# Preparing the quantised weight with fp32 matmuls on TensorE in place of GpSimd and VectorE arithmetic, in a one-core attention and feed-forward kernel

## The reference, cut to what matters

```
x = x + causal_attention(q = LN(x), k = ctx, v = ctx)          # 16 heads of 64
mask   = sigmoid(mask_weight)                                  # [4]
soft   = sigmoid(pweight) - sigmoid(nweight)                   # [1024 out, 1024 in, 4]
weight = einsum('oin,n->oi', soft, exps * mask) * scale[0]
bias   = quantise(einsum('on,n->o', pbias - nbias, bexps)) * biasscale[0]
x = x + LN(x) @ weight.T + bias
```

## Time and profile before

| what | value |
|---|---|
| median of 3 runs (lowest to highest) | 1310.44 us (1309.8 to 1312.69) |
| profiled execution, its own time | 1313.67 us |
| its span in the trace | 1310.7 us |
| mean granted TensorE clock, share of full speed | 0.944 |
| TensorE matmul busy (share of the span) | 1144.8 us (87%) |
| VectorE busy | 1072.6 us (82%) |
| ScalarE busy | 926.6 us (71%) |
| GpSimd busy | 599.9 us (46%) |
| read from memory, written to it | 67.15 MB, 16.78 MB |

### The profile page before, as it was taken

How to read it: one execution, slowest core, us unless ns; L and a number is a source line. 1 busy time by engine, 2 the same in 40 slices (tenths; PEclk the granted TensorE clock), 3 DMA queues, 4 the chain that set the end, 5 groups by cost and what they waited for, 6 DMA issues and landing times.

```text
span 1310.7 us, 28652 instructions
## 1 busy us (share of the span) xinstructions
PE 1144.8 (87%) x11088; PEld 848.5 (65%) x11088; DVE 1072.6 (82%) x1613; ACT 926.6 (71%) x2011; POOL 599.9 (46%) x717
## 2 busy tenths in 40 slices
PE   1555665589998999999999999999999999999998
PEld 1433444466766677777777677787776677777753
DVE  3588998878897688888898898888988888888861
ACT  1677787567776577777777777777787777777740
POOL 2378666533324574433324954433237744332241
PEclk9867767689999999999999999999999999999999
DMA  6899899243333675433324856434226854320113
GB/s 187 224 223 255 225 267 240 66 106 89 66 81 69 158 168 123 114 81 93 72 82 82 201 121 130 97 82 94 70 64 147 178 116 111 81 66 2 33 41 89
DMA packets 245622, 157.08 MB, mean 120 GB/s; under 512 B 220912, under 2 KB 220912, under 8 KB 245488
## 3 DMA queue, kind: packets, MB, share of 16 engines
q1 hardware_dynamic: 245488, 155.26, 49.5%
HBM read 67.15 MB, written 16.78 MB: 64 GB/s over the span
## 4 chain that ended last, share of the span: by engine, by line
PE 62%; DVE 19%; issue 6%; ACT 5%; POOL 3%; DMA 3%; SPq 1%; ACTq 0%; DVEq 0%; POOLq 0%
PE ffnb L433 20%; PE ptb L401 14%; PE oacc L415 7%; PE slot L388 7%; PE slot L389 7%; DVE pt_lo L570 5%; PE oacc L417 4%; DVE stats L584 3%; DVE mx L563 3%; ACT pt_hi L476 2%; PE slot L433 2%; PE slot L392 2%; DMA qt<-q 1%; DVE y L610 1%; DVE ring L619 1%
## 5 line engine op out<-in xcount | busy, mean ns | idle before, releaser
L570 DVE SCALAR_TENSOR_TENSOR pt_lo<-ptb,pt_hi 128x384 f16<-128x384 f32 (+2 forms) x688 | 382.9, 597 | 117.6 <-ACT pt_hi L476 115.4
L466 ACT ACTIVATE p<-slot,mx 128x512 f32<-128x512 f32 (+7 forms) x512 | 378.0, 747 | 96.1 <-DVE mx L563 94.1
L476 ACT ACTIVATE pt_hi<-ptb 128x384 f16<-128x384 f32 (+2 forms) x688 | 326.4, 527 | 150.2 <-PE ptb L401 149.4
L401 PE MATMUL ptb<-id,p 128*128 128x128 f32 x2304 | 340.8, 289 | 75.9 <-DVE pt_lo L570 75.0
L563 DVE TENSOR_REDUCE mx<-slot 128x1 f32<-128x640 f32 (+7 forms) x352 | 359.5, 1021 | 32.8 <-PE slot L392 30.2
L433 PE MATMUL ffnb<-wt,yt 128*128 128x512 f16 x1440 | 365.3, 381 | 18.6 <-DVE ring L619 15.6
L401 PEld LDWEIGHTS ptb<-id,p 128*128 128x128 f32 x2304 | 259.5, 146 | 87.6 <-issue 84.4
L388 PE MATMUL slot<-kt,qt 128*128 128x128 f16 (+3 forms) x1056 | 278.5, 293 | 38.8 <-DMA qs<-qt 26.5
L753 POOL TENSOR_TENSOR att<-osb 128x256 f32<-128x256 f32 x128 | 98.8, 772 | 398.9 <-ACT osb L483 375.8
L389 PE MATMUL slot<-kt,qs 128*128 128x128 f16 (+3 forms) x1056 | 278.4, 293 | 0.0
L415 PE MATMUL oacc<-v,pt_hi 128*128 128x128 f16 x2304 | 252.3, 224 | 15.3 <-ACT osb L483 13.4
(11 more groups left out here) (64 smaller groups left out, 976.8 us busy)
## 6 DMA issues: line engine op xcount, KB each, us to landing
ring<-in_x_dram SPq DMA_DIRECT2D x32, 512.0 KB, 4.9
cin<-in_ctx_dram SPq DMA_DIRECT2D x32, 512.0 KB, 4.2
qs<-qt SPq DMA_DIRECT2D x64, 256.0 KB, 3.8
out_dram<-ring SPq DMA_DIRECT2D x32, 512.0 KB, 2.9
v<-in_L_ffn_pweight_dram SPq DMA_DIRECT2D x16, 512.0 KB, 4.7
kt<-in_L_ffn_nweight_dram SPq DMA_DIRECT2D x16, 512.0 KB, 5.6
v<-in_L_ffn_nweight_dram SPq DMA_DIRECT2D x8, 512.0 KB, 7.6
kt<-in_L_ffn_pweight_dram SPq DMA_DIRECT2D x8, 512.0 KB, 4.5
```

The source lines that it names most:

```text
L401: last = pe.transpose(ptb[:, c % 2, at * P:(at + 1) * P], p32[:, j.par, k * P:(k + 1) * P], id32[:, :])
L466: last = nc.scalar.activation(p32[:, j.par, hh * j.keys:(hh + 1) * j.keys], slot[:, j.par, base:base + j.keys], ACT.Exp, bias=mx[:, j.par, ...
L476: nc.scalar.activation(pt_hi[:, j.par, P * blocks.start:P * blocks.stop], ptb[:, c % 2, 0:P * len(blocks)], ACT.Copy, scale=P_SCALE).then_ ...
L570: nc.vector.scalar_tensor_tensor(pt_lo[:, j.par, cols], ptb[:, c % 2, 0:P * len(blocks)], P_SCALE, pt_hi[:, j.par, cols], ALU.mult, ALU.su ...
```

## The change

The 32 chunks become 16 units of two chunks, one unit with each of jobs 0 to 15 (`UNITS = CHUNKS // 2`), and the buffer pairs become six. ScalarE's tanh on both halves stays. GpSimd's difference and VectorE's multiplication and sum go, and so does the DMA transpose. In their place TensorE computes, for each of a unit's four blocks of 128 x 128, eight fp32 matmuls that accumulate in `ffnb`: the stationary operand is one bit's plane of the tanh values (128 columns, every fourth fp32 element), the moving operand a 128 x 128 diagonal with that bit's coefficient, positive for pweight and negative for nweight. The result is the transposed block. ScalarE copies it from PSUM to the high part in `wt`, VectorE subtracts for the low part. Each is one instruction of 512 columns for a unit.

The eight coefficient diagonals are made on VectorE at the start. The feed-forward plan becomes one rule: tile t-4 with attention tile t, from t = 4 on, and the special steps for tiles 5 to 8 go. At the start, the first x and ctx tiles are loaded ahead of the small parameters, VectorE and ScalarE begin tile 0 ahead of the coefficient and bias work, the bias matmuls come after the scores of jobs 0 and 1 and use `oacc` and `ffnb`, and `bias_out` is waited for by the first weight unit and no longer by the first scores.

```diff
-PAIRS = 4
+UNITS = CHUNKS // 2
+PAIRS = 6
...
 def linear_plan(t):
-    n = steps(t) if t < TILES else 0
-    if t < 5:
-        return []
-    if t < 8:
-        return [(t - 5, 0, n)]
-    if t == 8:
-        return [(3, 0, n // 2), (4, n // 2, n // 2)]
-    return [(t - 4, 0, n)]
+    return [(t - 4, 0, steps(t))] if 4 <= t < TILES else []
...
-    late = {5: (6, 7, 9, 11), 6: (6, 7, 9, 11), 7: (6, 7, 9, 11), 8: (1, 2, 3, 3)}
-    return s == late.get(t, Q_STEPS[steps(t)])[part]
+    return t + 2 < TILES and s == Q_STEPS[steps(t)][part]
...
+        coef_diag = as_f32(yt, 1).rearrange("p (m q) -> p m q", m=2 * NBITS)
...
             def load_w(w):
-                reached(sp, w_sum, w - PAIRS + 1)
+                reached(sp, w_turned, (w - PAIRS) // 2 + 1)
...
-            def turn_w(o):
-                sp.wait_ge(w_lo, o + 1)
-                dst = wt[:, :, :, o * P:(o + 1) * P].rearrange("p a k c -> p (a k) c")
-                sp.dma_start_transpose(dst, y16[:, :, :, :].rearrange("p a k c -> p (a k) c")).then_inc(wt_in, 16)
...
+            load_x(0)
+            load_c(0)
             for at, src in ((0, exps), (4, bexps), (8, mask_weight), (12, scale), (13, biasscale)):
...
-            load_x(0)
-            load_c(0)
+            load_w(0)
             load_x(1)
-            load_w(0)
-            load_x(2)
-            load_w(1)
             turn_k(0)
             load_c(1)
+            load_w(1)
             turn_q(0)
             swap_q(0)
-            load_w(2)
             turn_k(1)
             load_c(2)
             turn_q(1)
+            load_w(2)
             load_w(3)
+            load_x(2)
+            load_w(4)
+            load_w(5)
...
                     for k in y_at(t, s, 2):
...
+                    u = FIRST[t] + s + 3
+                    if u < UNITS:
+                        load_w(2 * u)
+                        load_w(2 * u + 1)
                     if s == n - 1 and t + 2 < TILES:
                         turn_k(t + 2)
                         turn_q(t + 2)
...
+            def weights(u):
+                if u == 0:
+                    pe.wait_ge(coef_step, 2 * NBITS)
+                    pe.wait_ge(bias_out, 2)
+                reached(pe, w_lo, u)
+                pe.wait_ge(th_ready, 2 * u + 2)
+                for b in range(4):
+                    for m in range(2 * NBITS):
+                        a = pairs[(2 * u + b // 2) % PAIRS][m // NBITS].rearrange("p (k n) -> p k n", n=NBITS)
+                        last = pe.matmul(ffnb[:, b * P:(b + 1) * P], a[:, b % 2 * P:(b % 2 + 1) * P, m % NBITS],
+                                         coef_diag[:, m, :], start=m == 0, stop=m == 2 * NBITS - 1)
+                last.then_inc(w_turned, 1)
...
             for j in JOBS:
...
                 transpose_p(j)
+                if j.n < UNITS:
+                    weights(j.n)
...
+            def weights_high(u):
+                act.wait_ge(w_turned, u + 1)
+                nc.scalar.copy(wt[:, 0, u % 2 * 4:u % 2 * 4 + 4, u // 2 * P:(u // 2 + 1) * P],
+                               ffnb.rearrange("p (k c) -> p k c", c=P)).then_inc(w_hi, 1)
...
             for j in JOBS:
...
+                if 0 <= j.n - 1 < UNITS:
+                    weights_high(j.n - 1)
                 high_parts(j)
+                if j.n + 1 < UNITS:
+                    chunk_tanh(2 * j.n + 2)
                 if j.n + 2 < len(JOBS):
                     exponentials(JOBS[j.n + 2])
...
+                if j.n + 1 < UNITS:
+                    chunk_tanh(2 * j.n + 3)
...
-            def weights_sum(w):
-                a = pairs[w % PAIRS][0].rearrange("p (k n) -> p k n", n=NBITS)
-                dve.wait_ge(d_ready, w + 1)
-                nc.vector.tensor_tensor(a, a, coef.unsqueeze(1).to_broadcast([P, WCH, NBITS]), ALU.mult
-                                        ).then_inc(w_mul, 1)
...
-                nc.vector.tensor_reduce(w32[:, w % NWCH * WCH:(w % NWCH + 1) * WCH], a, AX_X, ALU.add
-                                        ).then_inc(w_sum, 1)
...
+            def weights_low(u):
+                dve.wait_ge(w_hi, u + 1)
+                rows, cols = slice(u % 2 * 4, u % 2 * 4 + 4), slice(u // 2 * P, (u // 2 + 1) * P)
+                nc.vector.tensor_tensor(wt[:, 1, rows, cols], ffnb.rearrange("p (k c) -> p k c", c=P),
+                                        wt[:, 0, rows, cols], ALU.subtract).then_inc(w_lo, 1)
...
-            def difference(w):
-                pool.wait_ge(th_ready, w + 1)
-                a, c = pairs[w % PAIRS]
-                nc.gpsimd.tensor_tensor(a, a, c, ALU.subtract).then_inc(d_ready, 1)
```

More of the change, by code:

```diff
@@ L241, in build @@
         bias_added, ffn_done, res_done = sem("bias_added"), sem("ffn_done"), sem("res_done")
-        th_ready, d_ready, w_mul, w_sum, w_hi, w_lo = (
-            sem("w_" + n) for n in ("tanh", "diff", "mul", "sum", "hi", "lo"))
+        th_ready, w_turned, w_hi, w_lo = (sem("w_" + n) for n in ("tanh", "turned", "hi", "lo"))
         pool_const, coef_tanh, coef_step, bias_step = (
@@ L331, in _ @@
                     if s == 0:
-                        if t >= 6:
-                            for k, _, _ in linear_plan(t - 1)[-1:]:
-                                store(k)
+                        if t >= 5:
+                            store(t - 5)
                         if t + 1 < TILES:
                             swap_q(t + 1)
[L337 to L351, removed]
+                    if s == n // 2 and t + 3 < TILES:
+                        load_x(t + 3)
                     if s == C_LO[n] and t + 3 < TILES:
@@ L436, in linear @@
                         last.then_inc(ffn_done, 1)
+            def weights(u):
[10 more added lines that the diff above has]
+                last.then_inc(w_turned, 1)
             pe.wait_ge(pool_const, 9)
+            scores(JOBS[0])
+            scores(JOBS[1])
             pe.wait_ge(bias_step, 18)
             for j in range(8):
-                last = pe.matmul(slot[:, 0, j * P:(j + 1) * P], ones32[:, :], bdiag[:, j, :], start=True, stop=True)
+                bank = oacc[:, j, :] if j < 4 else ffnb[:, (j - 4) * P:(j - 3) * P]
+                last = pe.matmul(bank, ones32[:, :], bdiag[:, j, :], start=True, stop=True)
             last.then_inc(bias_summed, 1)
-            scores(JOBS[0])
-            scores(JOBS[1])
             for j in JOBS:
@@ L518, in chunk_tanh @@
                 last.then_inc(th_ready, 1)
[L520 to L524, removed]
+            c_split(0)
             act.wait_ge(small_in, 16 * 7)
             nc.scalar.activation(coef, small[:, 8:12], ACT.Tanh, scale=0.5).then_inc(coef_tanh, 1)
+            q_split(0)
+            chunk_tanh(0)
+            c_split(1)
+            q_split(1)
+            chunk_tanh(1)
+            exponentials(JOBS[0])
+            exponentials(JOBS[1])
             act.wait_ge(bias_summed, 1)
             nc.scalar.copy(bias_row[:, :].rearrange("p (q j) -> p j q", j=8)[:, 0:4, :],
[L530 to L536, removed]
+                           oacc[:, :, :]).then_inc(bias_out, 1)
             for j in JOBS:
@@ L647, in bias_link @@
                 dve.wait_ge(bias_step, links[0])
+            q_moments(0)
+            c_split(0)
             dve.wait_ge(coef_tanh, 1)
@@ L652, in _ @@
             bias_link(nc.vector.tensor_scalar(coef, coef, small[:, 12:13], 0.5, ALU.mult, ALU.mult))
+            dve.wait_ge(pool_const, 9)
+            for m in range(2 * NBITS):
+                n = m % NBITS
+                nc.vector.tensor_scalar(coef_diag[:, m, :], id32[:, :], coef[:, n:n + 1],
+                                        1.0 if m < NBITS else -1.0, ALU.mult, ALU.mult).then_inc(coef_step, 1)
+            q_split(0)
+            q_moments(1)
+            c_split(1)
+            q_split(1)
             bias_link(nc.vector.tensor_tensor(bits[:, 0, :], bits[:, 0, :], bits[:, 1, :], ALU.subtract))
@@ L669, in _ @@
                     ins.then_inc(bias_step, 1)
+            maxima(JOBS[0])
+            maxima(JOBS[1])
             dve.wait_ge(bias_summed, 1)
             nc.vector.tensor_copy(bias_row[:, :].rearrange("p (q j) -> p j q", j=8)[:, 4:8, :],
-                                  slot[:, 0, 512:1024].rearrange("p (j q) -> p j q", j=4)).then_inc(bias_out, 1)
-            q_moments(0)
-            c_split(0)
-            q_split(0)
-            q_moments(1)
-            c_split(1)
-            q_split(1)
-            maxima(JOBS[0])
-            maxima(JOBS[1])
+                                  ffnb.rearrange("p (j q) -> p j q", j=4)).then_inc(bias_out, 1)
             for j in JOBS:
@@ L686, in _ @@
                     reciprocals(JOBS[j.n - 2].group)
+                if 0 <= j.n - 1 < UNITS:
+                    weights_low(j.n - 1)
                 low_parts(j)
-                w = weight_step(t, s)
-                if w is not None:
-                    weights(w)
                 for k in y_at(t, s, 2):
@@ L787, in _ @@
```

(3 more changed lines are left out.)

69 lines of the change are left out of this document (17 added, 52 removed).

## The result

The changed kernel takes 1417.8 us (median of 4 runs, 1416.42 to 1418.47), against 1310.59 us before (4 runs): 107 us longer, a ratio of 1.0814 with a 95% interval of 1.0795 to 1.0833. I had predicted 1273, with 1257 to 1335 as the range.

A forecast was written before the change was run, and what follows sets the result against it. VectorE and GpSimd bound the weight stage to about 263 us, PE the rest. Start 31.5 + units 148 + slips 3 = 182.5 us; job 96 at 422.2 against 459.97 gains 37.8: 1273 us, range 1257 to 1335.

The forecast's parts named there:

- the price of the fp32 matmuls: Weight units on PE: two records per fp32 matmul, 0.107 to 0.114 us apart, so 7.1 us a unit.
- Rival (a): Weight units: strided stationary loads double to 0.213 us and set PE's pace, +109 us, 1382 us in all; chance 0.20.
- second term: Between units: copy and subtraction freeing single-buffered `ffnb`, covered by attention and costed at nothing; uncovered, 1.3 us x 16 = 21.
- The decision point: Strided weight loads: slowdown per load above which the change would lose its gain, 37.8/1024 = 37 ns.
- The first exponentials: Start of the kernel: expected at 25 to 26 us against 36.71 before, with the first unit at 31.5 us.
- nearly the full clock: Weight stage: PE is busy for nearly all of each job, so its granted clock is 1.00 from about 40 us.
- light jobs: Jobs 18 to 24, with neither a unit nor a `linear`: 3.5 us each, bounds 3.0 and 5.0.
- tiles 4 to 9 as tiles 20 to 25: From tile 4 the plan equals that of tiles 20 to 25: 218.7 us, putting job 96 at 422.2.
- SyncE's queue: Weight stage: `load_w` waits for PE's units, with turns and swap behind it; 3 us allowed for slips and a low-clock first unit.
- (b): From 25 to 165 us DMA takes over: 300 GB/s needed; with 247 as the limit, 1302 us; chance 0.12.
- (c): Weight stage: PE's clock stays low for a quarter of the unit work, adding 27 us: 1300; chance 0.08.
- (d): Weight stage: ScalarE sets 10.5 us a job in place of 9.3, +19, 1292; within the main case's upper side.

The follow-up runs named there:

- the parts first: Changed kernel with ScalarE's high part ahead of the attention output and VectorE's low part ahead of maxima and reciprocals: 1400.83 us; with neighbouring elements too, 1281.93 us.
- the fastest version: Against the kernel with VectorE subtracting the tanh halves: difference written as two planes in own buffers, PE takes every second element, four load pairs: 1263.30 us.
- VectorE's difference: Against the changed kernel: high and low parts made first, VectorE subtracts the tanh halves, 16 fp32 matmuls a unit in place of 32: 1282.03 us.

## Why the prediction was wrong

The step that failed is the price of the fp32 matmuls. I took 0.107 to 0.114 us a record from rows whose stationary operands were contiguous; the strided one costs 0.233, so a unit took 14.9 us where the sum has 7.1. Rival (a) had the mechanism, its place and nearly its size: +109 us were said and 125 it was, since a load takes 0.233 us where I had doubled 0.107 to 0.213. The distance from this rival's 1382 us to the measured 1417.8 is about these 16 us, the 15.3 of the second term below and the 3.5 of the start. I gave it 0.20 because the one row on it was a write by another engine. That row was the only evidence on the operand's spacing in the whole trace, and nothing in the profile spoke against it but the general slowness of fp32; the bias matmuls, from which I took the price, said nothing of spacing. The decision point, 37 ns a load, was passed more than three times.

A second term was costed at nothing: the release of `ffnb`. I counted 1.3 us of copies against 1.5 to 2.4 us of attention, and overlooked that ScalarE's order puts `output` ahead, which waits for that same attention, so the attention hardly covers the copies. It cost 15.3 us in waits, and changing the order brought 17.0.

The first exponentials came 5.7 us earlier in place of 11. The first turn of the keys took the queue 6.09 us and that of the queries 5.48, where the kernel before has 1.80 and 2.85. So the queries' turn was issued at 15.76 us in place of 13 to 14, and ended 7.54 us later in place of 4.62. Now weight loads are in flight beside these turns. That they are the cause is not shown; the kernel before has one case like it, the second turn of the keys, issued right behind two weight loads, with 5.43 us.

The rest held: nearly the full clock (0.97 in both windows), light jobs at 3.5 us, tiles 4 to 9 as tiles 20 to 25, and neither SyncE's queue nor ScalarE as a bound at this pace. With neighbouring elements, at the pace that I had forecast, ScalarE and the DMA engines were no bound either: that run with the parts first takes 1281.93 us. Rivals (b), (c) and (d) did not decide. The 247 GB/s of (b) are no limit, since the fastest version moves 309.

## What to carry to other kernels

Before arithmetic is moved to TensorE, look at the spacing of its operands. Here a load of 128 fp32 elements took 1.8 ns for each 16 bytes that it spans from a spacing of two on, so every fourth element doubled the matmul's time and every second was nearly free. A pass of an idle engine that halves the number of matmuls, or packs the operand, paid at once: 119 and 19 us. When a buffer's release is said to be covered, read the releasing engine's program in order: what stands ahead of the release there, and what does that wait for? And where the only evidence for a rival is a distant row, but nothing stands against it, it deserves close to an even chance.

## What the runs showed of the hardware that I had not expected

A weight load that takes every fourth fp32 element takes 0.233 us at a granted clock of 0.50 as at 1.00, where 16-bit matmuls of 128 columns start 0.107 and 0.055 us apart. With 64 streamed columns in place of 128 the granted clock fell to 0.50 and 0.58 in windows where PE's records cover 95% and more. A stream of every fourth element costs nearly as much as such a load, 0.226 us. VectorE's difference, read and written in spread pairs, took about 1.22 us in 19 of 32 cases, as in place, but 1.74 to 1.75 us in eight, where none in place took over 1.49. On average it was 1.39 us against 1.26.
